# A decoder block on one core: expert tokens sorted and gathered by indirect transfers in place of masks

## The reference

```python
# 1: lightning attention, 16 heads of 16, in chunks of 128 tokens along s
#    o = (q k^T * decay) v  within the chunk  +  (q * decay) @ state of the chunk before
#    gate, rmsnorm by head, @ Wo
# 2: experts: F = 256, Wg = Wu = Wd = ctx[e]  (256 x 256)
expert_ids = jnp.minimum(jnp.clip(token_ids, 0, 12499) // 3125, 3)
for e in range(4):
    g = jax.nn.silu(jnp.einsum('bsd,fd->bsf', h, ctx[e]))
    u = jnp.einsum('bsd,fd->bsf', h, ctx[e])
    y = jnp.einsum('bsf,df->bsd', g * u, ctx[e])
    out = jnp.where((expert_ids == e)[..., None], y, out)
# 3: FFN with attention over the FOUR SEQUENCES at each position s (x is transposed to (s, b, d)):
#    u = silu(conv over b), q, k, v, g = projections of u, causal pair weights over b,
#    head norm, silu(g) * o, @ Wout
```

## Time and profile before

| | |
|---|---|
| median of 3 runs | 258.5 us (254.32 to 258.65) |
| span of the profiled execution | 256.0 us; its own time beside the span is not given, the median of the runs is 2.5 us above the span |
| PE, DVE, ACT, POOL busy | 209.2, 176.7, 81.7, 114.0 us |
| mean granted clock of PE | 0.925 of full |
| data moved by DMA | 6.65 MB |

### The profile page before, as it was taken

How to read it: one execution, slowest core, us unless ns; L and a number is a source line. 1 busy time by engine, 2 the same in 40 slices (tenths; PEclk the granted TensorE clock), 3 DMA queues, 4 the chain that set the end, 5 groups by cost and what they waited for, 6 DMA issues and landing times.

```text
span 256.0 us, 3809 instructions
## 1 busy us (share of the span) xinstructions
PE 209.2 (82%) x1254; PEld 146.0 (57%) x1254; DVE 176.7 (69%) x438; ACT 81.7 (32%) x219; POOL 114.0 (45%) x188
## 2 busy tenths in 40 slices
PE   3788999995987798849799989999999997842461
PEld 1367555562745364515799776686786966411340
DVE  1168848779597979793556863348769788897751
ACT  0075664452432534241100113403223234423021
POOL 9661207335161413140516352346558529656352
PEclk9999999999799999977979999999999999995555
DMA  7990000000000000000000000000000001001011
GB/s 195 339 299 5 3 0 4 0 1 0 3 1 0 3 1 0 3 0 0 3 0 3 1 0 0 3 1 0 0 3 0 0 4 40 3 0 41 0 38 45
DMA packets 7027, 6.65 MB, mean 26 GB/s; under 512 B 1232, under 2 KB 6624, under 8 KB 7008
## 3 DMA queue, kind: packets, MB, share of 16 engines
q1 hardware_dynamic: 5744, 5.33, 6.6%
q10 hardware_dynamic: 1264, 1.08, 1.4%
HBM read 5.36 MB, written 1.05 MB: 25 GB/s over the span
## 4 chain that ended last, share of the span: by engine, by line
PE 52%; DVE 24%; issue 9%; POOL 6%; ACT 4%; DMA 3%; ACTq 1%; DVEq 0%; POOLq 0%
PE bank L1029 19%; PE bank L1230 12%; PE bank L1087 9%; PE bank L1244 4%; PE bank L1024 3%; DMA w_qk<-in_L_attn_Wk 3%; DVE hTe L776 2%; DVE w_qk L937 2%; PE bank L1132 2%; DVE stats L749 1%; POOL rstd L301 1%; DVE newton L685 1%; DVE probs L717 1%; PE bank L1120 1%; DVE newton L684 1%
## 5 line engine op out<-in xcount | busy, mean ns | idle before, releaser
L1087 PE MATMUL bank<-qx,kT 128*128 128x512 f32 x64 | 33.7, 652 | 10.6 <-DVE probs L717 8.9
L1230 PE MATMUL bank<-hTe,ctxT 128*128 128x128 f32 x256 | 31.7, 285 | 2.6 <-issue 2.6
L1230 PEld LDWEIGHTS bank<-hTe,ctxT 128*128 128x128 f32 x256 | 31.0, 201 | 3.2 <-issue 3.1
L499 ACT ACTIVATE qx<-bank,con 32x256 f32<-32x256 f32 x64 | 26.4, 458 | 16.0 <-PE bank L1024 15.4
L1244 PE MATMUL bank<-ctxT,aTe 128*128 128x256 f32 x128 | 29.0, 379 | 0.0
L284 POOL TENSOR_TENSOR rsin<-qk,rope_tab 128x256 f32<-128x256 f32 x16 | 13.2, 845 | 34.9 <-ACT qk L482 34.9
L1029 PE MATMUL bank<-f_w,oT 128*128 128x512 f32 (+4 forms) x80 | 28.0, 496 | 0.8 <-ACT oT L552 0.7
L298 POOL TENSOR_SCALAR rstd<-agg 128x1 f32<-128x1 f32 x24 | 5.3, 222 | 49.3 <-DVE agg L751 48.5
L1087 PEld LDWEIGHTS bank<-qx,kT 128*128 128x128 f32 x64 | 11.7, 197 | 26.8 <-issue 24.5
L717 DVE TENSOR_TENSOR probs<-bank,con 128x512 f32<-128x512 f32 x32 | 21.6, 686 | 5.8 <-PE bank L1087 5.0
L1244 PEld LDWEIGHTS bank<-ctxT,aTe 128*128 128x128 f32 x128 | 23.7, 190 | 2.9
(11 more groups left out here) (128 smaller groups left out, 407.7 us busy)
## 6 DMA issues: line engine op xcount, KB each, us to landing
x_sb<-in_x SPq DMA_DIRECT2D x4, 256.0 KB, 6.8
ctx_sb<-in_ctx SPq DMA_DIRECT2D x1, 1024.0 KB, 12.3
out<-x_sb SPq DMA_DIRECT2D x8, 128.0 KB, 1.7
fgo<-in_itok_BxS ACTq DMA_DIRECT2D x1, 512.0 KB, 9.3
con<-shape_constants SPq DMA_DIRECT2D x1, 338.5 KB, 3.0
w_v<-in_L_attn_Wv SPq DMA_DIRECT2D x1, 256.0 KB, 5.5
w_qk<-in_L_attn_Wq ACTq DMA_DIRECT2D x1, 256.0 KB, 5.7
w_qk<-in_L_attn_Wk ACTq DMA_DIRECT2D x1, 256.0 KB, 7.3
```

Of the source, the lines that this page charges most:

```text
L499: eng.activation(qx[rr, i % 2, :, 2 * r + par, :], two(bank[2][rr, 0:2 * P]), ACT.Copy, scale=con[rr, C_PARITY + par:C_PARITY + par + 1]). ...
L1087: eng.matmul(bank[3 + g % 2][:, :], kT[:, i % 2, g // 2, :], qx[:, i % 2, g // 2, 4 * (g % 2):4 * (g % 2) + 4, :].rearrange("p h n -> p (h ...
L1230: last = eng.matmul(bank[0][:, f * P:(f + 1) * P], ctxT[:, k, e, f * P:(f + 1) * P], hTe[:, j % 2, e, k, :], start=(e == 0 and k == 0), st ...
```

## The change

- Tiles are now numbered by chunk: tile j is chunk j // 4, sequence j % 4. ORDER goes. The states of all four sequences are kept (state has a dimension b), made in rounds 0 to 3 and read for tiles 4 to 7.
- The masks and the masked copies go. Instead the tokens of each chunk (512) are sorted by expert into seven tiles of 128 rows ("slots"), each of one expert alone. Four experts with 512 tokens never need more than seven.
- Where each token goes is worked out in round 0: `mark_experts` (DVE, one-hot by expert), `rank_tokens` (PE, 8 small matmuls count the tokens ahead of each), `place_tokens` (DVE, some 15 operations, nearly all linked by a semaphore), in front of decay_state.
- POOL scatters each tile's normalized rows into a DRAM buffer by an indirect DMA (`scatter`), behind ln_rstd in rounds 3 to 7 and after. When four are in, SP loads the seven slots (`load_slots`, 896 KB). SP also copies each slot's weights from ctxT by a DMA whose source address is read from a register (`fetch_experts`, 256 KB each).
- The experts run by items of two slots (ITEMS, four per chunk, the last with one slot): turn_slots, copy_xsT, slots_up, silu_z, activate, slots_down, copy_ys, store_slots (to DRAM). When a chunk's four stores have landed, POOL gathers each tile's rows (`gather`, indirect), and residual2 adds them from SBUF.
- Every engine's list from round 7 on is written out anew: items 0 to 3 lie beside the end of attention, items 4 to 7 beside the FFN of chunk 0, and the FFN of chunk 1 follows. The lists of POOL, DVE and PE are shown below; ACT's runs silu_z(7), square_values(0), copy_ys(7) at the end of the experts.

The core of the diff:

```diff
+SLOTS = 7
+ITEMS = [(0, 2), (2, 4), (4, 6), (6, 7)]
...
+            def fetch_experts(c, s0, s1):
+
+                for s in range(s0, s1):
+                    e = eng.value_load(slot_e[0:1, c, s:s + 1], min_val=0, max_val=E - 1)
+                    eng.dma_start(slot_w[:, s, :, :], ctxT[:, bass.ds(e, 1), :, :].rearrange("p o k n -> p (o k) n"))\
+                       .then_inc(S_(f"slot_w{c}{s}"), 16)
+
+            def load_slots(c):
+
+                eng.wait_ge(S_(f"scattered{c}"), 16 * L)
+                if c:
+                    eng.wait_ge(S_("xsT_made"), len(ITEMS))
+                eng.dma_start(xs[:, :, :], xs_d[c][:, :].rearrange("(s q) d -> q s d", q=P)).then_inc(S_("xs_in"), 16)
+
+            def store_slots(c, m):
+
+                s0, s1 = ITEMS[m]
+                n = len(ITEMS) * c + m
+                eng.wait_ge(S_("ys_copied"), n + 1)
+                eng.dma_start(ys_d[c][s0 * P:s1 * P, :].rearrange("(s q) d -> q s d", q=P),
+                              ys[:, n % 2, 0:(s1 - s0) * D].rearrange("p (s d) -> p s d", d=D))\
+                   .then_inc(S_(f"ys_stored{c}{m}"), 16)
+
+            eng.wait_ge(S_("slots_known"), 1)
+            eng.wait_ge(S_("ctxT_copied"), E)
+            fetch_experts(0, 0, SLOTS)
+            load_slots(0)
+            for m in range(len(ITEMS)):
+                store_slots(0, m)
+                fetch_experts(1, *ITEMS[m])
+            load_slots(1)
+            for m in range(len(ITEMS)):
+                store_slots(1, m)
...
+            def scatter(j):
+
+                c, l = j // L, j % L
+                if l == 0:
+                    eng.wait_ge(S_("pos"), 1)
+                    eng.wait_ge(S_("xs_zeroed"), 32)
+                eng.wait_ge(S_("h1_done"), j + 1)
+                eng.indirect_dma_start(xs_d[c][:, :], bass.IndirectOffsetOnAxis(ap=pos[:, l, c:c + 1], axis=0),
+                                       h1[:, j, :], None).then_inc(S_(f"scattered{c}"), 16)
+
+            def gather(j):
+
+                c, l = j // L, j % L
+                if l == 0:
+                    for m in range(len(ITEMS)):
+                        eng.wait_ge(S_(f"ys_stored{c}{m}"), 16)
+                if c:
+                    eng.wait_ge(S_("ln1_sum"), l + 1)
+                eng.indirect_dma_start(yg[:, l, :], None, ys_d[c][:, :],
+                                       bass.IndirectOffsetOnAxis(ap=pos[:, l, c:c + 1], axis=0))\
+                   .then_inc(S_(f"y_back{j}"), 16)
...
+            for i in range(TILES):
+                attention_round(i)
+            scale_o(6)
+            scatter(5)
+            ln_rstd(0, 6)
+            scale_o(7)
+            scatter(6)
+            ln_rstd(0, 7)
+            scatter(7)
+            for l in range(L):
+                gather(l)
+            for l in range(L):
+                ln_rstd(1, l)
+            route_weights(0)
+            weigh_values(0)
+            route_weights(1)
+            gate_values(0)
+            weigh_values(1)
+            scale_values(0)
+            gate_values(1)
+            scale_values(1)
+            for l in range(L):
+                gather(L + l)
+            for l in range(L):
+                ln_rstd(1, L + l)
+            root_of_last(0)
+            root_of_last(1)
+            route_weights(2)
...
+            def place_tokens():
+
+                eng.wait_ge(S_("ranked"), 1)
+                rank = bank[6][:, 0:TILES * E].rearrange("p (b c e) -> p b c e", b=B, c=2)
+                total = bank[6][:, TILES * E:TILES * E + 2 * E].rearrange("p (c e) -> p c e", c=2)
+                link(eng.tensor_scalar(tiles_of[:, :, :], total, 0.0, None, ALU.is_gt))
+                for k in range(1, L):
+                    link(eng.scalar_tensor_tensor(out=tiles_of[:, :, :], in0=total, scalar=float(k * P),
+                                                  in1=tiles_of[:, :, :], op0=ALU.is_gt, op1=ALU.add))
+                link(eng.tensor_scalar(first[:, :, 0:1], tiles_of[:, :, 0:1], 0.0, None, ALU.mult))
+                for e in range(1, E):
+                    link(eng.tensor_tensor(first[:, :, e:e + 1], first[:, :, e - 1:e], tiles_of[:, :, e - 1:e], ALU.add))
+                link(eng.scalar_tensor_tensor(out=ranks[:, :, :, :],
+                                              in0=first[:, :, :].unsqueeze(1).to_broadcast([P, B, 2, E]),
+                                              scalar=float(P), in1=rank, op0=ALU.mult, op1=ALU.add))
+                link(eng.tensor_tensor(ranks[:, :, :, :], ranks[:, :, :, :], onehot[:, :, :, :], ALU.mult))
+                link(eng.tensor_reduce(pos_f[:, :, :], ranks[:, :, :, :], AX.X, ALU.add))
+                eng.tensor_scalar(pos[:, :, :], pos_f[:, :, :], -1.0, None, ALU.add).then_inc(S_("pos"), 1)
+                link(eng.tensor_tensor(before[:, :, :, :],
+                                       count[:, 0:SLOTS].unsqueeze(1).unsqueeze(1).to_broadcast([P, 2, E - 1, SLOTS]),
+                                       first[:, :, 1:E].unsqueeze(3).to_broadcast([P, 2, E - 1, SLOTS]), ALU.is_ge))
+                link(eng.tensor_reduce(slot_f[:, :, :], before[:, :, :, :].rearrange("p c e s -> p c s e"), AX.X, ALU.add))
+                eng.tensor_copy(slot_e[:, :, :], slot_f[:, :, :]).then_inc(S_("slots_known"), 1)
...
+            activate(0)
+            residual1(5)
+            gate_o(6)
+            norm_o(6)
+            activate(1)
+            scale1(5)
+            gate_o(7)
+            residual1(6)
+            norm_o(7)
+            activate(2)
+            scale1(6)
+            activate(3)
+            residual1(7)
+            scale1(7)
+            residual2(0)
+            residual2(1)
+            scale2(0)
+            conv_step(0)
+            scale2(1)
+            residual2(2)
+            residual2(3)
+            scale2(2)
+            scale2(3)
+            activate(4)
+            conv_step(1)
+            activate(5)
+            pair_dots(0)
+            pair_weights(0)
+            conv_step(2)
+            weigh_pairs(0)
+            weigh_values(0)
+            activate(6)
+            sum_values(0)
+            conv_step(3)
+            head_var(0)
+            head_rstd(0, 0)
+            activate(7)
+            pair_dots(1)
+            pair_weights(1)
+            weigh_pairs(1)
+            weigh_values(1)
+            sum_values(1)
+            head_var(1)
+            head_rstd(1, 1)
+            residual2(4)
+            residual2(5)
+            scale2(4)
+            residual3(0)
+            conv_step(4)
+            scale2(5)
+            residual2(6)
+            conv_step(5)
+            residual2(7)
+            scale2(6)
+            scale2(7)
+            residual3(1)
+            conv_step(6)
+            pair_dots(2)
+            pair_weights(2)
+            weigh_pairs(2)
+            weigh_values(2)
+            conv_step(7)
+            sum_values(2)
+            pair_dots(3)
+            pair_weights(3)
+            weigh_pairs(3)
+            weigh_values(3)
+            head_var(2)
+            head_rstd(2, 2)
+            sum_values(3)
+            pair_dots(4)
+            pair_weights(4)
+            weigh_pairs(4)
+            weigh_values(4)
+            head_var(3)
+            sum_values(4)
+            residual3(2)
+            head_var(4)
+            head_rstd(3, 4)
+            residual3(3)
+            residual3(4)
...
+            def rank_tokens():
+
+                flat = onehot[:, :, :, :].rearrange("p b c e -> p (b c e)")
+                n, m = TILES * E, 2 * E
+                eng.wait_ge(S_("ones"), 1)
+                eng.wait_ge(S_("onehot"), 3)
+                eng.wait_ge(S_("xT_copied"), TILES)
+                eng.matmul(bank[6][:, 0:n], causal, flat, start=True, stop=False)
+                for b in range(1, B):
+                    eng.matmul(bank[6][:, b * m:n], ones[:, :], flat[:, 0:n - b * m], start=False, stop=(b == B - 1))
+                for b in range(B):
+                    last = eng.matmul(bank[6][:, n:n + m], ones[:, :], flat[:, b * m:(b + 1) * m],
+                                      start=(b == 0), stop=(b == B - 1))
+                last.then_inc(S_("ranked"), 1)
...
+            def slots_up(n):
+
+                c, m = n // len(ITEMS), n % len(ITEMS)
+                s0, s1 = ITEMS[m]
+                eng.wait_ge(S_("xsT_copied"), n + 1)
+                if n:
+                    eng.wait_ge(S_("activated"), n)
                 else:
                     eng.wait_ge(S_("qk_silu"), TILES)
-                for f in range(KT):
-                    for e in range(E):
+                for q in range(s0, s1):
+                    eng.wait_ge(S_(f"slot_w{c}{q}"), 16)
+                    for f in range(KT):
+                        a = (2 * (q - s0) + f) * P
                         for k in range(KT):
-                            last = eng.matmul(bank[0][:, f * P:(f + 1) * P],
```

(69 more changed lines are left out.)

627 lines of the change are left out of this document (279 added, 348 removed).

## The result

The changed kernel takes 275.3 us (median of 4, 273.05 to 276.1), the kernel before 256.4 (4 runs, 254.32 to 258.65): 1.075 times the time, with a 95% interval of 1.065 to 1.084. The profiled execution took 274.79, of which 272.4 is the span. The forecast was 270.5. It was built on the 256.0 us of span before: it said 12 us more span, and 16.4 were measured. (The three runs before had a median of 258.5; with a fourth it is 256.4.)

The account below looks back on a forecast made before the run. The prediction took PE to bound the middle and a chain through four engines the end. h2 starts 4 us later, then 116 us instead of 108: 256 + 12 = 268 of span, plus 2.5 for the median, 270.5 us; range 253 to 284.

Parts of the forecast that it names:

- PE saves 30 us: Experts on PE: 56.3 us of matmuls become 24.7, transposes grow by 1.3, so PE saves 30 us.
- (a): Routing in round 0: rank_tokens and place_tokens make the second roped tile late, +2.2 us, bounds 0 and 5.
- The four state matmul pairs and the four state reads only change rounds: nothing.: Attention rounds: state matmuls and reads move to other rounds, at a cost of nothing.
- (b): Indirect transfers on POOL: issue 1.2 us each, landing 2.0; five scatters in rounds 3 to 7 cost nothing.
- (d): First round trip: store, four gathers, then the h2 work; project_step(0) starts at 153.5, PE idles 9.5 us.
- (c): Experts of chunk 0, beside attention of tiles 6 and 7: slots_down(3) ends at 142.3.
- (e): Chunk 0's FFN with chunk 1's items: up(7) ends at 186.6; chunk 1's gathers, behind pair group 1, at 207.0.
- (f): Second round trip: gathers 4.8 us, then rstd, scale2, residual3(0), conv and silu; project_step(4) starts at 216.2.
- (g): Last four steps of chunk 1's FFN: project_step(7) ends at 239.5, the span at 267.7.
- Rival 2: Whole kernel: PE's time counts and the end moves by PE's saving, 240 us, milder form 250; chance 0.13.
- Rival 4: Indirect transfers are dear on POOL, 2.5 us each, giving 284; chance 0.14.
- Rival 3: No change: POOL issue, landing, routing and half clock each at the low end, giving 258; chance 0.17.

Follow-up runs that it names:

- 6: Changed kernel with place_tokens moved from the end of round 0 to the end of round 1, behind mask_scores; span 275.1, ratio 1.088.
- 9: Changed kernel with unread matmuls in PE's waits in rounds 3, 4 and 6 and ahead of transpose_h2(0) and transpose_h2(4); span 267.1, ratio 1.053.
- 11: Kernel of 10 plus unread matmuls in PE's waits in the rounds and ahead of transpose_h2(0) and transpose_f(0); span 258.6, ratio 1.015.
- experiment 4: Changed kernel with SP's load of chunk 1's slots held until two chunk 0 gathers landed, turn_slots(4) behind project_step(0); span 273.7, ratio 1.073.
- Experiment 2: Changed kernel with activate(7) ahead of head_var(0) and chunk 1's gathers ahead of pair group 1's work, other queues reordered accordingly; span 262.5, ratio 1.034.
- 5: Changed kernel with the first scatter moved from round 3 to round 4, ahead of the second one; span 268.8, ratio 1.055.
- 1: Changed kernel with activate(7) moved ahead of head_var(0) and head_rstd(0, 0) on DVE; span 272.9, ratio 1.065.
- 3: Changed kernel without chunk 0's gathers, leaving its experts' part out of the result, project_step(0) ahead of turn_slots(4); span 267.5, ratio 1.046.
- 8: Changed kernel with 24 unread 128x512 matmuls on PE ahead of transpose_h2(0) and 11 ahead of transpose_h2(4); span 279.2, ratio 1.097.
- 10: Changed kernel with the orders of Experiment 2 and 5, plus transpose_f(1), project_out(1), copy_fT(1), residual3(1) behind project_step(6); span 265.4, ratio 1.038.

## Why the prediction was right, and where it was off

The time (270.5 against 275.3) and the mechanism held: the round trips and the orders of POOL and DVE put waits where PE's work had been. Part of the closeness is luck. project_step(0) came 7.1 us later than forecast and the end 4.4 to 4.7, because later terms erred the other way. Of the signs that the prediction named, the gathers' spacing (1.26 us), the half clock behind both gaps and the idle time ahead of transpose_h2(0) (12.0) came. The gap ahead of transpose_h2(4) was 7.6 us where it said 8 or more, the first gather of chunk 1 came 10 us behind the landing and not 12, PE was 21 us less busy and not 30, and round 7 was 6.5 us later and not 2. The terms, in order:

- **PE saves 30 us.** 21 less busy. The matmuls that went are as counted (14 slots, 1066 records instead of 1254). Of the 9 us between, 1.7 are rank_tokens, which the 30 left out; the rest is the same work at a lower clock, 0.876 on average instead of 0.925.
- **(a) Routing, +2.2.** Round 1 was 2.7 later, of which 0.7 before round 0; round 0 starts anywhere from 23.7 to 25.5 us in the traces of this section, so that part may be chance. The size held, the reason not: I put it on place_tokens on DVE and added nothing for rank_tokens. 6 shows that DVE's part is worth 0.2 there, and the rows that PE has 1.7 us more.
- **"The four state matmul pairs and the four state reads only change rounds: nothing."** This is the step that failed, with nearly the whole error: round 7 was forecast at 109.1 and came at 113.4. PE's work in rounds 4 and 6 fell, and its wait for the masked scores grew, from 1.40 to 4.33 us in round 4 and from 1.04 to 2.81 in round 6. Round 4's wait, before and after:

```profile
78.18 1.96 PE L1087 MATMUL bank<-qx,kT 128*128 128x512 f32 x4 [1.40 <-DVE probs L717]
```

```profile
80.78 3.75 PE L1248 MATMUL bank<-qx,kT 128*128 128x512 f32 x4 [4.33 <-DVE probs L857]
```

  Both parts of round 4, before and then after, split where PE's wait ends:

```profile
67.65:78.18 10.53, 7.92 (x86) 5.04 (x84) 9.71 (x29) 4.77 (x11) 6.78 (x13) 1.00 0.00 1
78.18:81.79 3.61, 3.57 (x14) 2.18 (x15) 2.43 (x4) 0.38 (x1) 0.00 (x0) 1.00 0.00 0
```

```profile
69.52:80.78 11.26, 6.34 (x49) 3.31 (x48) 10.45 (x27) 4.76 (x11) 7.36 (x14) 0.91 0.04 14
80.78:86.46 5.68, 5.68 (x14) 3.34 (x15) 2.44 (x4) 0.38 (x1) 0.00 (x0) 0.58 0.00 0
```

  The same 14 PE records take 3.57 us and then 5.68, at a clock of 0.58: 2.1 of the 2.8 us. The other 0.7 is DVE, which lies beside POOL's work that the scatter pushed back. Round 6 lost 1.4 to the clock in the same way. 9 shows it: with the waits filled, the rounds are back at 14.9 and 13.4 (14.1 and 13.3 before), and 11, with the scatter moved as well, has 14.2 in round 4. That the missing state matmuls are what made the waits long enough is read from these rows; no run put the matmuls back.
- **(b) Scatters nothing, gathers 1.2 each, landing 2.0.** Issues 0.95 to 1.27 us, at a spacing of 1.26: right. The scatters were not free in their effect, but with either sign: one in round 4 cost 0.7 us there, by what it pushed beside DVE's chain; one in round 5 left 12.15 us (11.76 before), and two made it 10.99. Issue and landing together, 3.2 forecast, were 2.6 (experiment 4) and 2.9 (second trip) without other traffic and 5.3 beside the load. That puts 2.6 us on **(d)**: project_step(0) at 160.6 instead of 153.5, with 4.5 inherited. From the first gather to transpose_h2(0) it took 8.0 us where 6.0 were forecast, and 6.2 in experiment 4, so 1.8 of it are the load, which the prediction had put down as done by then; another 0.5 lies ahead of the gather. By the Trainium skill, "DMA: Bandwidth & Descriptors", section "Anatomy of one DMA — SWDGE (gpsimd) path", one such transfer takes 2.3 us, an estimate from its fit; that is near the 2.6 alone and far from the 5.3 beside the load.
- **(c) Experts of chunk 0.** From round 7 to the end of slots_down(3) 33.2 us were forecast and 33.4 measured.
- **(e)** The end of up(7) was 7 us late, as inherited; from there to the gather 20.4 were forecast and 19.0 measured. **(f), (g)** and the end were 5.3, 5.1 and 4.7 late, nothing new in them. The 1.7 us for the half clock behind each gap, for which the prediction gives no row, was right in size: project_step(0) and (4) took 5.90 and 6.18 us, and 4.19 with the gaps filled. What the prediction lacked was the same price behind the short waits of rounds 4 and 6.
- **Rival 2 (PE's time counts)** failed on its stated condition: up(7) ended at 193.5, not before 172, and the gathers started at 212.5, not before 192. Experiment 2 moved them to 200.6 and won 10 us, a third of what PE saves. **Rival 4**: an issue of 2.5 us didn't occur. **Rival 3** needed all unknowns at their low ends, and of these only the landing was near it (2.6 to 2.9 us with 1.0 to 1.1 of issue in it).

So of the 16.4 us of span by which the change is slower, the order at the second trip is 9.9 and the half clock, where 9 filled it, about 5; with the better orders, the fills and the scatter moved, the span is 20.0 shorter than the changed kernel's. These effects overlap (the clock falls behind waits that the orders make), so they don't add up exactly.

What stays open: why the same code in the same place falls to half clock in one execution and not in the next (below), and how much of the gain in 5 was its doing.

## What to carry to other kernels

When a change takes work from the bounding engine, look for the places in which that engine now waits, and count the slow time behind each wait as well as the wait. When a result comes back through a queue that other work shares, put its issue at the earliest place at which it can be ready: here the order was worth 10 us, nearly twice what the gathers of the other trip cost. An operation that is moved costs by what it then stands beside, so read the neighbours at the new place, not only the idle time there.

## What the runs showed of the hardware

- The granted clock after a wait differs between executions of the same instructions. Round 3 is the same code in the changed kernel and in 1, 3, 4 and 8, and PE waits the same 2.1 us in it; it took 12.86 us in the first and 14.55, 14.22, 14.54 and 14.39 in the others, with the clock of its last stretch at 1.00 in the one and at 0.64 and 0.61 in 1 and 3. That is 1.7 us of noise from one place, of which round 4 gave back up to 0.7 (16.94 us in the first, 16.27 in 1).
- Matmuls that nobody needs, put into PE's waits, kept the clock full behind them and shortened the kernel: by medians 275.3 to 269.5 us (9), and 266.7 to 260.5 (11 against 10). Where they ended 2.1 to 2.3 us before the wait did, the step behind ran at half clock all the same (project_step(4) in 9, project_step(0) in 11). The Trainium skill, "TensorE: Matmul & The Clock Gate", section "Part 1: The HAM clock gate", puts the penalty of the ramp, in a passage on a kernel's start, below 1% of a typical kernel's span. The drops inside this kernel are another matter: the fills of 9 gave 2% (5.3 of 272.4).
- An indirect gather of 128 KB took 2.6 and 2.9 us from issue to use alone and 5.3 beside a load of 896 KB.
